# GNN kernel on one core: both one-hot matrices of an attention step from one VectorE comparison, GpSimd issues only the gathers

## The reference

```
h = relu(layernorm(x));  x = x + GNN(h)       # mean over neighbours, two dense products, batch norm
h = relu(layernorm(x));  x = x + ATTN(h)
ATTN: Q, K, V = h@Wq, h@Wk, h@Wv, in 8 heads of 64
      score[e,h] = exp(clip(sum_d K[src]*Q[dst] / 8, -5, 5))
      wV = segment_sum(V[src]*score, dst);  Z = segment_sum(score, dst)
      h + wV/(Z+1e-6), then batch norm over the nodes
```

## Time and profile before

| | |
|---|---|
| median of 3 runs | 3966.51 us (3964.63 to 3968.85) |
| span of the profiled execution | 4129.4 us |
| busy share of the span: PE, DVE, ACT, POOL | 83%, 58%, 43%, 61% |
| attention loop: first and last gather issued | 2288.0 and 3867.7 us |
| aggregation loop: gathers, from about | 387 to 1698 us |
| data moved | 827.43 MB, of which 615.66 MB by the gathers' queue |

### The profile page before, as it was taken

How to read it: one execution, slowest core, us unless ns; L and a number is a source line. 1 busy time by engine, 2 the same in 40 slices (tenths; PEclk the granted TensorE clock), 3 DMA queues, 4 the chain that set the end, 5 groups by cost and what they waited for, 6 DMA issues and landing times. The chain is left out here.

```text
span 4129.4 us, 67061 instructions
## 1 busy us (share of the span) xinstructions
PE 3416.5 (83%) x11730; PEld 1994.7 (48%) x11731; DVE 2394.5 (58%) x4270; ACT 1769.0 (43%) x7008; POOL 2502.5 (61%) x2615
## 2 busy tenths in 40 slices
PE   4998877778787787749999799999999999999750
PEld 3885433334333343328888455555555555555310
DVE  3443111111111111465554798999999999999999
ACT  1332000000000000232222788888888888888620
POOL 0002666666666666421111788888888888888656
PEclk9999888898899888979999999999999999999965
DMA  2334555555555555435555788888888888888537
GB/s 72 130 131 132 154 155 153 155 154 157 155 159 158 152 155 157 141 107 210 209 204 203 249 277 272 277 277 276 275 275 277 276 279 277 274 276 274 178 106 217
DMA packets 292261, 827.43 MB, mean 200 GB/s; under 512 B 57891, under 2 KB 57893, under 8 KB 292202
## 3 DMA queue, kind: packets, MB, share of 16 engines
q0 software_dynamic: 197504, 615.66, 47.6%
q1 hardware_dynamic: 87710, 198.68, 14.7%
q10 hardware_dynamic: 7020, 12.80, 0.8%
HBM read 993.99 MB, written 116.36 MB: 269 GB/s over the span
## 5 line engine op out<-in xcount | busy, mean ns | idle before, releaser
L604 POOL DMA_INDIRECT rows<-y_d,idx x880 | 886.8, 1008 | 779.3 <-DVE rows L618 352.1
L1017 ACT ACTIVATE kv<-kv,wgt 128x64 f32<-128x64 f32 x4400 | 1097.9, 334 | 0.0
L658 PE MATMUL pss<-rows,hot 128*128 128x512 f32 x1760 | 969.4, 681 | 144.4 <-issue 114.6
L984 POOL DMA_INDIRECT kv<-kv_d,idx x880 | 932.4, 1059 | 208.8 <-issue 203.3
L1141 PE MATMUL psa<-kv,hot 128*128 128x512 f32 x1760 | 867.7, 616 | 95.4 <-DVE parts L1069 35.6
L1061 DVE TENSOR_TENSOR kv<-kv,ps_q 128x1024 f32<-128x1024 f32 x440 | 534.8, 1215 | 131.4 <-DMA kv<-kv_d,idx 86.5
L579 ACT COPY idx<-src_t 128x4 int32 (+1 forms) x224 | 43.0, 193 | 1282.1 <-DMA rows<-y_d,idx 1265.8
L658 PEld LDWEIGHTS pss<-rows,hot 128*128 128x128 f32 x1760 | 335.5, 212 | 411.4 <-issue 410.3
L1074 DVE TENSOR_REDUCE score<-kv 128x16 f32<-128x1024 f32 x440 | 531.9, 1209 | 0.0
L1129 PE MATMUL ps_q<-q,hotT 128*128 x1760 | 521.2, 418 | 7.4 <-issue 2.9
L1141 PEld LDWEIGHTS psa<-kv,hot 128*128 128x128 f32 x1760 | 302.6, 189 | 446.7 <-issue 440.6
(11 more groups left out here) (168 smaller groups left out, 3778.5 us busy)
## 6 DMA issues: line engine op xcount, KB each, us to landing
q<-q_d SPq DMA_DIRECT2D x440, 512.0 KB
q_d<-q_sb SPq DMA_DIRECT2D x49, 512.0 KB, 2.7
kv_d<-o_sb SPq DMA_DIRECT2D x49, 512.0 KB, 3.9
x_sb<-in_x SPq DMA_DIRECT2D x96, 256.0 KB, 2.9
rows<-y_d,idx POOLq DMA_INDIRECT x880
kv<-kv_d,idx POOLq DMA_INDIRECT x880
y_d<-o_sb SPq DMA_DIRECT2D x49, 256.0 KB, 2.0
z_d<-o_sb SPq DMA_DIRECT2D x49, 256.0 KB, 2.3
```

What stands on the lines that cost most here:

```text
L604: pool.indirect_dma_start(rows[:, u, g, :], None, y_d[0:N, :], bass.IndirectOffsetOnAxis(idx[:, u // H, k:k + 1], 0), bounds_check=limit, ...
L658: nc.tensor.matmul(pss[:, ds(par, D)], hot[:, u, g, :].bitcast(F32), rows[:, u, g, :], start=False, stop=(g == G - 1), skip_group_check=True)
L984: pool.indirect_dma_start(kv[:, u, g, :], None, kv_d[0:N, :], bass.IndirectOffsetOnAxis(idx[:, u // H, k + g:k + g + 1], 0), bounds_check= ...
L1017: last = nc.scalar.mul(v, v, wgt[:, u, g * HEADS + h:g * HEADS + h + 1])
```

## The change

Line numbers in the diff are those of the kernel before. POOL's comparisons, the staging copy `rel` and its tile, the semaphore `hot_made_dve` and the waits for it go. `one_hot` on DVE runs in every step and writes both groups' matrices with one comparison of 128x256. It reads `rel_t` itself, at an address that depends on the step, and so no longer waits for `staged`. Before it restages, ACT now waits only for the rows of the two steps.

```
--- before.py
+++ after.py
@@ -914,13 +914,12 @@
                 parts = sb(ctx, "parts", [P, 4, G, 2, HEADS], F32R)
                 idx = sb(ctx, "idx1", [P, U // H, H * G], I32)
                 ps_q = [pb(ctx, f"ps_q{k}", [P, G * D]) for k in range(2)]
-                rel = sb(ctx, "rel1", [P, U // H, H * G])
                 ps_h = pb(ctx, "ps_h", [P, 512])
                 pss = pb(ctx, "psa", [P, 2 * D])
                 psc = pb(ctx, "psw", [P, 512])
                 cleared_by, staged, rows_in, q_in = sems("cleared1_", 2), sem("staged1"), sems("rows_in1_", U), sems("q_in", QB)
-                hot_made, hot_made_dve, turned, copied, expanded, multiplied = (
-                    sem("hot_made1"), sem("hot_made_dve1"), sem("hot_turned"), sem("hot_copied"), sem("expanded"), sem("multiplied"))
+                hot_made, turned, copied, expanded, multiplied = (
+                    sem("hot_made1"), sem("hot_turned"), sem("hot_copied"), sem("expanded"), sem("multiplied"))
                 reduced, clipped, weighed, by_act, by_dve = (
                     sem("reduced"), sem("clipped"), sem("weighed"), sem("scaled_by_act"), sem("scaled_by_dve"))
                 ps_made, high = sem("ps_made1"), sem("weights_high")
@@ -976,10 +975,6 @@
                             pool.wait_ge(ps_made, i * U + u + 1)
                             alone(pool)
                             k = (u % H) * G
-                            for g in range(1 + u % 2):
-                                last = nc.gpsimd.tensor_scalar(hot[:, u, g, :], lane[:, :], rel[:, u // H, k + g:k + g + 1], None,
-                                                               ALU.is_equal)
-                            last.then_inc(hot_made, 1)
                             for g in range(G):
                                 pool.indirect_dma_start(kv[:, u, g, :], None, kv_d[0:N, :],
                                                         bass.IndirectOffsetOnAxis(idx[:, u // H, k + g:k + g + 1], 0),
@@ -997,7 +992,6 @@
 
                         def stage(i, part):
                             at = ds((i * U + part * H) * G, H * G)
-                            nc.scalar.copy(rel[:, part, :], rel_t[:, at])
                             nc.scalar.copy(idx[:, part, :], src_t[:, at]).then_inc(staged, 1)
 
                         def copy_hot(s, i, u):
@@ -1020,8 +1014,6 @@
                         def restage(i, part):
                             for u in range(part * H, part * H + H):
                                 act.wait_ge(rows_in[u], 16 * G * (i + 1))
-                            act.wait_ge(hot_made, (i * (U // H) + part + 1) * H)
-                            act.wait_ge(hot_made_dve, i * (U // H) + part + 1)
                             alone(act)
                             stage(i + 1, part)
 
@@ -1050,9 +1042,9 @@
 
                         def one_hot(s, i, u):
                             dve.wait_ge(ps_made, s + 1)
-                            dve.wait_ge(staged, (s // H if isinstance(s, int) else i * (U // H) + u // H) + 1)
-                            nc.vector.tensor_scalar(hot[:, u, 1, :], lane[:, :], rel[:, u // H, (u % H) * G + 1:(u % H) * G + 2],
-                                                    None, ALU.is_equal).then_inc(hot_made_dve, 1)
+                            nc.vector.tensor_tensor(hot[:, u, :, :], lane[:, :].unsqueeze(1).to_broadcast([P, G, P]),
+                                                    rel_t[:, ds(s * G, G)].unsqueeze(2).to_broadcast([P, G, P]),
+                                                    ALU.is_equal).then_inc(hot_made, 1)
 
                         def multiply(s, i, u):
                             dve.wait_ge(rows_in[u], 16 * G * (i + 1))
@@ -1091,7 +1083,7 @@
                                 scale(*step)
                             if step := steps(i, u, 0):
                                 reduce(*step)
-                            if (step := steps(i, u, 3)) and step[2] % 2 == 0:
+                            if step := steps(i, u, 3):
                                 one_hot(*step)
                             if step := steps(i, u, -1):
                                 flush(*step)
@@ -1112,8 +1104,6 @@
 
                         def turn(s, i, u):
                             pe.wait_ge(hot_made, s + 1)
-                            if u % 2 == 0:
-                                pe.wait_ge(hot_made_dve, i * (U // 2) + u // 2 + 1)
                             pe.wait_ge(copied, s + 1)
                             for g in range(G):
                                 last = nc.tensor.transpose(ps_h[:, g * P:(g + 1) * P], hot[:, u, g, :].bitcast(F32), ident[:, :])
```

More of the change, by code:

```diff
@@ L978, in fetch @@
                             k = (u % H) * G
[L979 to L982, removed]
                             for g in range(G):
```

## The result

The changed kernel takes 3869.38 us (median of 4 runs, 3869.19 to 3872.23) against 3966.88 for the one before: 0.9755, with a 95% interval of 0.974 to 0.9769. It is 97.5 us **faster**. The forecast was 3995, with 3918 as the lower end of its range, so both sign and range were wrong.

A forecast was written before the change was run, and what follows sets the result against it. POOL was taken to pace the attention loop at 1577 us, 1512 in runs after removing 65 us of recorder time; with the change DVE would pace it at 1541, so +29 us gave 3995, range 3918 to 4035.

The forecast's parts named there:

- POOL sets the pace of the kernel before: Attention loop: POOL's comparisons and gathers, worked without a break, set its step of 3.585 us.
- four fifths of the 163 us on the 1760 gathers: Both edge loops: the recorder lengthens each gather by 0.074 us, 65 us in the attention loop, absent in runs.
- break-even of 0.04 us a gather: Both edge loops: the recorder's lengthening of a gather at which the change would neither gain nor lose.
- rival 1: Attention loop: the profile holds in the runs, POOL costs 3.585 us a step there too, 36 us gain, 3930; chance 0.24.
- DVE's new work, +0.19 us a step: Attention loop: the 128x256 comparison adds 0.16 or 0.23 us to DVE's step, mean 0.19, 85 us in all.
- The address: Attention loop: DVE's sequencer computes the operand's step-dependent place in rel_t, covered by the reduction; costed at nothing.
- I take 0.05: Attention loop: DVE's clip and scaling, stretched beside POOL, get back 0.05 us a step; bounds nothing and 0.16.
- rival 2: Attention loop: POOL's comparisons caused the stretching, 0.16 us a step returns, DVE's line 3.325; 3882 to 3948; chance 0.08.
- the 1541 us of the sum: Attention loop after the change: DVE's line of 3.435 us, 1511 us for 440 steps, plus 30 of waits for PE.
- Waits, 30 us: Attention loop: DVE's waits for PE rise from 20.4 to 30 us as the slack between them shrinks.
- POOL waits for buffers: Attention loop: without comparisons POOL needs about 2.7 us a step, then waits for buffers and is off the path.
- Rival 3: Attention loop: gathers hold DVE's comparison up to 502 ns, adding 34 us, about 4030; chance 0.10.

The follow-up runs named there:

- the two kernels without and with its comparisons: The kernel before with POOL's comparisons left out, none in their place: 3842.42 us; the changed kernel with them added back beside DVE's: 4003.63 us.
- the second profile: The kernel before, unedited, profiled once more: 3967.58 us, with a span of 3965.7 us.
- the small comparison on it: The changed kernel with one comparison of 64 elements a step added on POOL ahead of the gathers: 3872.72 us.
- The fall from 375 to 309 ns with the form: The kernel with one comparison a step on each of POOL and DVE, DVE's written as tensor_tensor instead of tensor_scalar: 3863.55 us against 3868.37.
- The kernel with 0.5 comparisons a step: The kernel before with POOL making one comparison in odd steps only, DVE the others: 3862.35 us.

## Why the prediction was wrong

- **POOL sets the pace of the kernel before**: right. Its step of 3.585 us, its wait of 4.6 us for buffers and the order of the timeline said so, and so do the two kernels without and with its comparisons.
- **The step that turned the sign: "four fifths of the 163 us on the 1760 gathers"**, +65 us on the changed kernel's side of the balance. It measured zero: the second profile, with the same gathers of 998 ns, has a span within 2 us of the runs. The excess lay in one execution's aggregation loop, outside the change. I had the evidence: the page's row of PE's granted clock, by fortieths of the span, has 8 in nine of the twelve slices of that loop (the 5th to the 16th) and 9 in the attention loop. Before, and then the changed kernel:

```profile
PEclk9999888898899888979999999999999999999965
```

```profile
PEclk8999999999999999979999999999999999999865
```

  The remark that DVE's durations leave the recorder no room was right and told nothing of gathers. Without this term my sum gave 36 us of gain, 3930, faster and inside the range. The break-even of 0.04 us a gather, and the test by span against runs, were put rightly; rival 1, the profile holding in the runs, got 0.24.
- **DVE's new work, +0.19 us a step**: right within 0.02. The comparison occupies 0.33, against 0.19 (+0.14) and against the gap of 0.12 ahead of the clip (+0.21). Read by starts, the way from the reduction to the clip grew by 0.17. The address cost nothing, as said.
- **"I take 0.05" for the stretching that ends**: mis-sized. DVE's line is 3.366 - 0.043 of waits = 3.323 us, so 0.16 came back, the upper bound, as rival 2 had it (3.325). I weighed by how much of the time gathers and comparisons fill. That was the wrong measure: beside gathers without comparisons in POOL's queue the clip takes 177 ns and the scaling 553. The 0.11 between, over 440 steps, is 48 us, and with the 11 us of the next point it is the distance from the 1541 us of the sum to the 1481 measured.

  What the 0.16 is made of is not clean, because a long record of the clip can cover time in which the product waited anyway. In 424 steps of the loop before, 224 clips took over 0.25 us. In 73 of these steps the product started within 0.13 us of the clip's start, as if nothing were held, and in 96 it started only after the clip had ended. From the scaling's start to the next instruction's, 0.04 us came back. From the clip's start to the product's it was 0.35 (0.49 before, 0.14 after), 0.25 of it idle time and 0.10 under the clip's record. How much of this 0.10 was delay by the hold, and how much waiting for rows, no run shows.
- **Waits, 30 us**: 19.1 measured. Those for PE fell from 20.4 to 9.5 us, instead of rising.
- **"POOL waits for buffers"**: it waits for the staged indices from ACT (324.7 us) and hardly for the sums (18.1). For the time it is the same: POOL is off the path, as the small comparison on it shows.
- **Rival 3**, DVE's comparison held up by the gathers: fell. It takes 413 ns, never over 419. The rule that I quoted from the Trainium skill (SBUF — State Buffer, "Who interferes with whom") speaks of GpSimd instructions that read SBUF. In the changed kernel this case shows nothing of it beside gathers. Beside POOL's comparisons, which read SBUF, it agrees in part. In the kernel before, 102 of 424 scalings took over 0.6 us, up to 0.92, and 94 of these overlapped a comparison on POOL, of the other 322 only 146; with no comparisons there, no scaling took over 625 ns. With POOL comparing beside the changed DVE, the low part of the weights took over 0.2 us in 233 of 424 steps, 221 of them beside a comparison (2 of the other 191), while the scaling stayed at 551 ns although 340 overlapped one.

The ledger of the 97.5 us, by the steps: 0.29 of waits fall to 0.04 (-0.25), comparison +0.18 or 0.19, stretching (with what its records cover) -0.16, together -0.22 us, 96 us over the loop.

## What to carry to other kernels

Before the difference between a profiled span and the runs goes into a sum, find the stretch in which it lies: compare the granted clock and the pace of each loop, and profile the kernel before twice if that can be had. Look for the engine that never waits: here it was POOL, busy 86%, that set the pace, and not PE or DVE with 94% and 92%. How much to move off that engine is then set by the next one's pace: here moving a third of POOL's comparisons gave all of the gain, and leaving a third of them on POOL was 7 us better still.

## What was unexpected of the hardware

DVE's small tensor_scalars are often held until the end of a gather on POOL where comparisons stand in POOL's queue and it works almost without a break, and less often elsewhere. In the first profile of the kernel before, 222 of the 432 clips from 2300 to 3850 us took over 0.25 us, and 157 of these ended within 0.1 us of the end of a gather. For example (the gather ends at 2437.95, the clip at 2437.93, and the product starts all the same 0.10 after the clip's start):

```profile
2436.87 1.08 POOL L984 DMA_INDIRECT kv<-kv_d,idx  x1 [0.17 <-issue]
2437.47 0.46 DVE L1080 TENSOR_SCALAR score<-score 128x16 f32<-128x16 f32 x1
2437.57 1.22 DVE L1061 TENSOR_TENSOR kv<-kv,ps_q 128x1024 f32<-128x1024 f32 x1
```

For the clip this is all but absent with gathers alone (177 ns), with comparisons and slack on POOL (171), and where DVE's big comparison stands ahead of the clip (184). For the 128x128 comparison it is not: with gathers alone a fifth of them were still held to a gather's end.

The same section of the Trainium skill (SBUF — State Buffer, "Who interferes with whom") says that a DVE tensor_scalar can take the port pair that it shares with GpSimd, for a whole instruction, and that a tensor_tensor has no such mode. The fall from 375 to 309 ns with the form agrees with that. The kernel with 0.5 comparisons a step does not quite: there 25 of 212 tensor_tensors of 128x256 took over 0.46 us, and all 25 ended within 0.1 us of the end of a gather. Why the hold is so much more frequent where POOL has comparisons in its queue and no slack, no run here settles.
